# A decoder of two layers on one core: router step in three parts, roots of the low-rank rows on GpSimd, a new order table

## What is computed

```
x = LN(x + latent_attention(x))          # 32 heads, low-rank q (192) and kv (64), rotary part 64, causal
x = LN(x + mix of x with top-76-of-256 masked similarities of the context)
x = LN(x + experts(x))                   # 7 routed experts + 1 shared, top 2 of 7 by router
x = LN(x + attention(x))                 # 16 heads of 16, rotary, causal
x = LN(x + softmax(LN(sim)*gamma+beta))  # bilinear similarity with the context
x = LN(x + down(silu(gate(x)) * up(x)))  # hidden 1024
```

```
# first attention: RMS norm of the low-rank rows
q   = rms_norm(x @ q_a_w) @ q_b_w            # x * rsqrt(mean(x*x) + 1e-6) * w
ckv = rms_norm((x @ kv_a_w)[..., :64])
# router of the experts
gate = x @ Wr + br
_, ids = top_k(gate + gate_bias, 2)
masked = full(-inf); masked[ids] = gate[ids]
probs = softmax(masked)
```

## Time and profile before

| what | value |
| --- | --- |
| three runs | 713.79, 714.95, 715.62 us |
| the profiled execution | 713.86 us, of which the span from first to last instruction is 712.0 us |
| TensorE, matmuls | 686.8 us busy (96%), 4886 |
| VectorE | 539.4 us (76%), 1701 instructions |
| ScalarE | 496.5 us (70%) |
| GpSimd | 389.1 us (55%), 647 instructions |
| chain that ended last | TensorE 82%, VectorE 8%, GpSimd 3% |

### The profile page before, as it was taken

One profiled execution on the slowest core, in us unless ns is written; L12 is line 12 of the kernel. 1 busy time (PEld: TensorE's weight loads), 2 busy tenths in 40 slices (PEclk: granted clock), 3 DMA queues, 4 the chain that ended last, 5 costly groups with the idle time before them and its releaser, 6 DMA issues.

```text
span 712.0 us, 14718 instructions
## 1 busy us (share of the span) xinstructions
PE 686.8 (96%) x4886; PEld 576.6 (81%) x4886; DVE 539.4 (76%) x1701; ACT 496.5 (70%) x1277; POOL 389.1 (55%) x647
## 2 busy tenths in 40 slices
PE   8899999999999999999987999999989999999995
PEld 6577898889888888889875988888967777768885
DVE  4967899887788969888878956566788778749464
ACT  4787865888568684888877867665756676876641
POOL 4269642885267731878965546834781321336652
PEclk9999999999999999999999999999999999999998
DMA  8671001140431302212021002210120000010301
GB/s 286 172 227 34 16 1 45 46 120 1 124 114 37 114 2 65 54 33 61 1 90 46 1 0 90 77 58 1 45 89 3 4 2 4 3 46 1 122 27 45
DMA packets 34419, 41.06 MB, mean 58 GB/s; under 512 B 6620, under 2 KB 27238, under 8 KB 34344
## 3 DMA queue, kind: packets, MB, share of 16 engines
q1 hardware_dynamic: 33800, 39.80, 19.0%
q10 hardware_dynamic: 544, 0.33, 0.1%
HBM read 30.02 MB, written 1.05 MB: 44 GB/s over the span
## 4 chain that ended last, share of the span: by engine, by line
PE 82%; DVE 8%; POOL 3%; issue 2%; SPq 2%; ACT 1%; DMA 1%; POOLq 0%; DVEq 0%
PE bank L1181 72%; PE bank L1195 10%; SPq L2625 1%; DVE top_tok L2258 1%; DVE router_buf L1891 1%; POOL w_split_lo L2361 1%; POOL probs L2361 1%; POOL stat L2361 1%; DMA qT<-xT_plain 1%; DVE y L1894 1%; POOL qT L2361 0%; ACT x L1593 0%; DVE bn L1926 0%; DVE key_tok L1894 0%; DVE xT_lo L1894 0%
## 5 line engine op out<-in xcount | busy, mean ns | idle before, releaser
L2358 POOL TENSOR_SCALAR probs<-probs,soft 128x256 f32<-128x256 f32 (+1 forms) x256 | 105.7, 437 | 51.3 <-DVE soft L2054 49.8
L1681 ACT ACTIVATE probs<-probs,soft 128x256 f32<-128x256 f32 (+1 forms) x256 | 113.0, 447 | 15.1 <-DVE soft L2046 14.7
L1181 PE MATMUL bank<-xT_hi,w_split_hi 128*128 128x512 f32 x256 | 104.0, 406 | 2.5 <-POOL w_split_lo L2361 1.4
L2361 POOL TENSOR_TENSOR w_split_lo<-w_raw,w_split_hi 128x512 fp32r<-128x512 f32 (+2 forms) x57 | 73.0, 1289 | 52.3 <-ACT w_split_hi L1586 48.3
L1181 PE MATMUL bank<-xT_lo,w_split_hi 128*128 128x512 f32 x256 | 100.6, 393 | 0.0
L2046 DVE CUSTOM_DVE_ANT_0 probs<-bank,mask 128x256 f32<-128x256 f32 (+1 forms) x256 | 78.8, 353 | 25.6 <-PE bank L1181 23.7
L1181 PE MATMUL bank<-keyT,qT 128*128 128x256 f32 (+1 forms) x512 | 93.5, 330 | 2.7 <-POOL qT L2361 2.7
L1181 PEld LDWEIGHTS bank<-keyT,qT 128*128 128x128 f32 x512 | 81.9, 190 | 14.7 <-POOL qT L2361 4.8
L2361 POOL TENSOR_TENSOR qT<-qT,xT_plain 64x512 f32<-64x512 f32 x44 | 56.0, 1273 | 53.8 <-DMA qT<-xT_plain 51.6
L1181 PE MATMUL bank<-xT_hi,w_split_lo 128*128 128x512 f32 x192 | 75.7, 394 | 0.0
L1586 ACT ACTIVATE qT<-bank 64x512 f32<-64x512 f32 (+1 forms) x80 | 47.3, 593 | 29.7 <-PE bank L1181 26.3
(11 more groups left out here) (245 smaller groups left out, 1814.5 us busy)
## 6 DMA issues: line engine op xcount, KB each, us to landing
qT<-xT_plain SPq DMA_DIRECT2D x88, 64.0 KB, 2.0
w_raw<-in_w_nopeT SPq DMA_DIRECT2D x8, 512.0 KB, 3.7
w_raw_heads<-in_w_o SPq DMA_DIRECT2D x8, 512.0 KB, 5.4
qT<-rope_buf SPq DMA_DIRECT2D x40, 64.0 KB, 2.0
w_raw<-in_w_gateT SPq DMA_DIRECT2D x8, 256.0 KB, 2.7
w_raw<-in_w_upT SPq DMA_DIRECT2D x8, 256.0 KB, 3.1
w_raw<-in_w_downT SPq DMA_DIRECT2D x8, 256.0 KB, 3.7
w_raw<-in_L_ffn_Wup SPq DMA_DIRECT2D x7, 256.0 KB, 2.7
```

The source lines that it names most:

```text
L1181: return t.matmul(out, lhsT, rhs, start=start, stop=stop, skip_group_check=shared)
L1681: ins = s.activation(p[:, at], p[:, at], ACT.Exp, bias=st[:, 0, r:r + 1], scale=-1.0, accum_out=st[:, 1, r:r + 1])
L2358: return g_.tensor_scalar(out, in0, s1, s2, op0, op1)
L2361: return g_.tensor_tensor(out, in0, in1, op)
```

## The change

1. ("down_root", h): VectorE only adds the epsilon (signal `low_seeded`). GpSimd takes the power -0.5 of 8 columns and makes one Newton round of four instructions, and signals `low_rsqrt`. The step has a place in GpSimd's order, and `power` is 8 columns wide.
2. The router: the part after the top-8 search is a step of its own, ("route_pick", h), so that other steps can stand between the three parts. The second mask is added with -1 in the same instruction, and one scalar_tensor_tensor replaces the tensor_scalar and the add of route_soft: one instruction less for each half, two in all.
3. The planner's costs for these steps, `NEAR` and the table `URGENT` are new, so that every engine's order changes.
4. The two signals of the last statistics are merged with the others; their order in time is as before.

```diff
-    NEAR = {"PE": 0.0, "ACT": 0.3, "DVE": 0.3, "POOL": 0.3, "SP": 0.5, "DMA": 0.05, "WAY": 0.0}
+    NEAR = {"PE": 0.0, "ACT": 0.3, "DVE": 0.3, "POOL": 0.5, "SP": 0.3, "DMA": 0.1, "WAY": 0.0}
...
-        ("adj_T", 0): -24, ("adj_mask", 2): 70, ("adj_mask", 3, 1): 17, ("adj_sim", 2): 45, ("adj_top", 1): 362,
+        ("adj_mask", 2, 1): 49, ("adj_top", 1): 241, ("adj_top", 2): 86, ("adj_top", 3): 133, "adj_top": -33,
...
-        stage(("down_root", h), "DVE 2.7", ("down", h))
+        stage(("down_root", h), "DVE 0.2, POOL 2.2", ("down", h), ("zero",))
...
-        stage(("route_gate", h), "PE 0.5, DVE 2.7", ("route_lin", h),
+        stage(("route_gate", h), "PE 0.5, DVE 1.8", ("route_lin", h),
               holds=[bank("route_gate", h, left=(("route_gate", h), "DVE"))])
-        stage(("route_soft", h), "DVE 0.9, ACT:exp 0.3", ("route_gate", h))
+        stage(("route_pick", h), "DVE 2.2", ("route_gate", h))
+        stage(("route_soft", h), "DVE 1.8, ACT:exp 1.5", ("route_pick", h))
...
-                own(seed(ve, r, sums[:, h, :, :].rearrange("p a t -> p (a t)"), 1e-6))
-                newton_steps(ve, r, s_).then_inc(low_rsqrt.sem, 1)
+                ts(stat[place][:, 0, :], sums[:, h, :, :].rearrange("p a t -> p (a t)"), 1e-6, None, ALU.add).then_inc(low_seeded.sem, 1)
...
-                tt(pick, pick, other, ALU.add).then_inc(route_picked.sem, 1)
+
+                stt(pick, pick, -1.0, other, ALU.add, ALU.add).then_inc(route_picked.sem, 1)
...
-                own(ts(tmp, pick, -NEG, NEG, ALU.mult, ALU.add))
-                w.wait_ge(*own.now)
-                own(tt(tmp, tmp, gate, ALU.add))
+                own(stt(tmp, pick, -NEG, gate, ALU.mult, ALU.add))
...
+        def newton_step(r, s, ve):
+            w.wait_ge(*own.now)
+            own(tt(s, r, r, ALU.mult))
+            w.wait_ge(*own.now)
+            own(tt(s, s, ve, ALU.mult))
+            w.wait_ge(*own.now)
+            own(ts(s, s, -0.5, 1.5, ALU.mult, ALU.add))
+            w.wait_ge(*own.now)
+            return tt(r, r, s, ALU.mult)
...
+            elif name == "down_root":
+                h, = k
+                ve, r, s_ = (stat[in_stat.place["down", h]][:, j, :] for j in range(3))
+                w.wait_ge(*zeroed["zero"])
+                w.wait_ge(*low_seeded[h])
+                own(tt(r, ve, power[:, :], ALU.pow))
+                newton_step(r, s_, ve).then_inc(low_rsqrt.sem, 1)
```

137 lines of the change are left out of this document (54 added, 83 removed), and 41 rows, old and new, of the table URGENT.

## The result

The changed kernel takes 703.82 us (median of four runs, 702.86 to 705.43) where the kernel before took 714.37 on the same chip (713.26 to 715.62): ratio 0.9854, 95% interval 0.9828 to 0.988. Run once more on another chip it took 705.07 against 713.43, ratio 0.988 (0.9854 to 0.9905). Its profiled execution took 705.43 us with a span of 703.6 us, 8.4 less than the span of before.

What follows compares the result with a forecast made beforehand. TensorE's matmuls were taken as the bound, busy 686.8 of 712.0 us. Terms -4.2 (router), -1.2 (GpSimd's run), 0 (start), 0 (rest) sum to -5.4 us: 708.5 profiled, median 709.6, range 706.0 to 715.5.

Steps and rivals of the forecast that it cites:

- The router, -4.2: Router of half 0: xT_lo ahead of route_soft removes TensorE's 2.6 us wait and 1.7 us of low clock; -4.2 us.
- rival A: Router: the hole only moves, something else holds e_u(2,1); only GpSimd's 1.2 us left, median 713.7 us; chance 0.14.
- the new wait: Router: TensorE would wait 0.2 us for u_pair_lo, ready at 384.8 us.
- GpSimd's run, -1.2: Before the second attention: a split moved into GpSimd's idle time shortens TensorE's 1.69 us wait for q_rows; -1.2 us.
- ScalarE is late next: Before the second attention: the bound of 0 gain, if ScalarE, which makes the high part first, is late next.
- The start, 0: Roots and SP's queue: root ready as late as before, query waits may go (-2.3) or grow (+2); taken as 0.
- B: Start: SP's ten loads hold the first query beyond about 35 us; +1.7 to +3.4 us, median up to 718.3; chance 0.11.
- D: Start: GpSimd's root instructions wait for VectorE's, each root 1.8 us late, twice; -1.8 us in all, median 713.2; chance 0.07.
- C: Start: VectorE's freed 5.6 us lets first queries be evicted earlier, both query waits go; -7.7 us in all, median 707.3; chance 0.10.
- The rest of the order, 0 with a bound of -1: Some 450 steps changing places where TensorE's windows are full: 0 us, bounds -1 and +2.5.
- the price of the low clock at the router: Behind the xT_lo wait, four 1 us windows at low granted clock lack 1.7 us of full speed.

Runs made afterwards that it cites:

- fused_only: The kernel before with only the two router instructions fused away, one less per half, and nothing moved: 711.49 us against 713.38, ratio 0.9977.
- split_pair: The kernel before with the 512-wide split (17, 0) put ahead of the 1536-wide (16, 0) on ScalarE and GpSimd: 713.18 us against 713.38, ratio 0.998.
- root_on_vector: The changed kernel with the root of the low-rank rows back on VectorE and out of GpSimd's order: 705.29 us against 713.87 for the kernel before, ratio 0.9875.
- start_new: The changed kernel's instructions, its order up to about 95 us and the old order behind: 711.29 us against 713.38 for the kernel before, ratio 0.997.
- half_new: The changed kernel's instructions, its order up to the experts' end, the old order from the second attention on: 706.45 us against 713.38 for the kernel before, ratio 0.9902.
- weights_first: The changed kernel with split (10, 0) ahead of e_gate (0, 0) on ScalarE and GpSimd: 705.2 us against 713.43 for the kernel before, ratio 0.9884.
- late_new: The changed kernel's instructions, its order at the start and from the second attention on, the old order between: 707.49 us against 713.38 for the kernel before, ratio 0.9911.
- After_again: The changed kernel run once more, unchanged, on another chip: 705.07 us against 713.43 for the kernel before, ratio 0.988.
- att_new: The changed kernel's instructions, its order up to the norms behind the first attention, the old order from there: 711.36 us against 713.38 for the kernel before, ratio 0.995.
- tokens_late: The kernel before with ctx_tok's 16 small products moved later on TensorE, and their copy on VectorE: 712.94 us against 713.65, ratio 0.9983.
- xT_first: The kernel before with one VectorE step moved, batch 3's xT_lo ahead of route_soft of half 0: 710.53 us against 713.38, ratio 0.9953.

## Why the prediction was wrong, step by step

**The router, -4.2: nearly right.** The xT_lo wait and the low clock went as forecast; the step is 3.3 us in after and 3.5 for the move alone, and rival A did not come. The part mis-sized is the new wait: 0.2 forecast, 0.96 measured. I charged VectorE for GpSimd's run but not GpSimd for VectorE's: its products took 3.45 instead of 2.51 us, so the next router instruction was held as well (1.28 us). I also put the saved instruction to nothing beyond this sum. Alone the fusion is worth 2.8 us in the old order (fused_only), since it takes the wait to 1.37 us, and behind that the clock did not fall. Move and fusion cover the same hole: undoing the move costs 0.7 us with the fusion there, undoing both 1.9.

**GpSimd's run, -1.2: wrong, -0.3.** split_pair shows the step that failed: I took GpSimd's run to be bound by GpSimd alone. GpSimd also waits for VectorE's rope_tmp, 0.99 us there and 0.95 in after; the bound that I gave for "ScalarE is late next" had the right form, and VectorE was the one.

**The start, 0: near, and in part by luck.** The root is 3.1 us from the add to its end, as estimated (11.46 to 14.57), the power 1.66 and 1.85 us for an estimate of 1.7; the first query goes out at 28.38 us for a forecast 28.6; root_on_vector finds the place of the root worth nothing, which agrees with the Trainium skill (Perfetto Trace Analysis, Optimizing Scalar/DVE Operations), by which moving work between these two engines might not help. The traces of after are 0.5 and 1.8 us ahead by 348 us, and traces with the old start scatter by 1.4. The luck is in the clock: none of the six traces with the old start has it low between 14 and 75 us, six of the nine with after's start have, near 24 or 47 us, which costs 1.7 us each. The three without it (start_new, half_new, weights_first) are 1.1 to 2.4 us ahead by 348 us. So the new start takes waits away and mostly pays with the clock; I had priced neither. TensorE has 10.25 of 12 us between 36 and 48 us, its least between 24 and 60, where under 9.5 would have been the sign of B, and the first query goes out well before the 35 us of B; D's late root did not come either. Of C's two waits both went, but a new one of 1.75 us for qT came at 45.56, so C did not come as priced.

**The rest of the order, 0 with a bound of -1: the step that failed, 4.4 us.** "The largest holes of the old order outside the places above are these waits of 1.4 to 1.7 us, so I take 0": this looked for large holes in full windows. There were a wait of 1.27 us at 360.82, one of 0.74 at 373.2, and the five between 529 and 559 us. half_new gains 2.2 us at the first two, late_new 2.4 at the others and behind them, of which 0.3 is GpSimd's run. Each could have been looked up: in the listing of the new order ctx_tok stands where the hole of 1.27 us was. Which step closes each wait is shown for none of them. The sum by the traces is then -0.5 - 2.1 - 3.3 - 0.2 - 1.8 - 0.6 = -8.5, against -8.4 of the spans; without the start, the router and the 0.3 it is the 4.4 of this term.

**The clock of single executions: the last 0 to 2 us.** Executions of one kernel differ in the mean clock, and the time goes with it. Mean clock and span of seven of the 92 executions of before on record beside the experiments, and the four of after:

```
before  0.998 709.7   0.997 709.4   0.995 711.0   0.994 711.1   0.992 714.0   0.990 714.0   0.987 717.6
after   0.999 701.0   0.998 701.6   0.996 702.4   0.994 703.6
```

Over all 92 a thousandth of the clock goes with 0.68 us. 81 of them have a mean clock of 0.997, 0.995, 0.992, 0.990 or 0.987, steps of some 2.5 thousandths, which is 1.7 us of 712: an estimate from these numbers is that they count stretches like that of the earlier trace rows. The profiled execution of after was its slowest: behind the 1.75 us wait at 45.56 its clock fell, and in half_new, the same order there, behind a wait of 1.3 us it did not. The windows of after, then of half_new:

```profile
44.00:48.00 4.00, 2.44 (x12) 2.30 (x13) 1.18 (x7) 1.30 (x6) 3.76 (x7) 0.84 0.91 265
48.00:52.00 4.00, 4.00 (x17) 3.36 (x16) 2.98 (x12) 1.93 (x7) 3.84 (x7) 0.74 0.58 192
```

```profile
44.00:48.00 4.00, 2.76 (x17) 2.51 (x18) 1.79 (x10) 1.75 (x7) 3.82 (x6) 1.00 0.93 299
48.00:52.00 4.00, 4.00 (x22) 3.27 (x22) 3.60 (x18) 3.39 (x10) 3.84 (x8) 1.00 0.50 151
```

Where the stretches lie differs between executions. After_again has its own not at 47 but at 25 us:

```profile
24.00:28.00 4.00, 3.29 (x9) 2.58 (x10) 1.17 (x2) 2.07 (x5) 3.60 (x6) 0.65 0.33 68
```

Behind the q_rows wait of the second attention three of the nine traces with the old order there have one (start_new, att_new, tokens_late), 1.4 to 1.8 us each, and none of the eleven with the new order. So the new order of that stage can win more in the median than the 1.8 us, which are against an execution without it.

The mean clock is 0.9939 over the 24 executions of before beside xT_first and 0.997 over the nine of xT_first: by the 0.68 us that is 2.1 us, near the 1.7 that the four windows of the earlier trace rows lacked. So the price of the low clock at the router was right.

## What to carry to other kernels

Where a new order is part of the change, go through every wait of the old one above 0.3 us and look up in the listing what now stands before it: the waits that looked too small to price held more gain than the one that was priced. Where two edits close one hole their gains don't add up, and each is to be priced with and without the other; a move that clears a wait shows the next engine that is late (ScalarE, the other queries) at nearly the same size. Count in how many executions the clock is low at a place before you take one trace for the kernel, and look whether a kernel with the old order shows the same gain before you give it to a move. In an order this tight, five tries with one to three moves each found nothing more.

## What the runs showed of the hardware

VectorE and GpSimd hold each other: two g_pair_lo 2.93 us instead of 1.28, the two GpSimd products beside them 3.45 instead of 2.51. How the same two instructions fall together changes with the execution: 1.93 or 0.88 us for y. One instruction on 128x32, 0.19 us alone, is worth 1.22 us beside a run of GpSimd, shown by taking it out (wait 2.59 to 1.37 us).

A power of 8 columns on GpSimd takes 1.66 and 1.85 us.

The granted clock of the same place differs between executions: 0.72 at 516 to 520 us in start_new behind its 1.7 us wait for q_rows, 1.00 in before behind the same wait. A wait of 1.4 us for xT_lo at the router had no low clock behind it in any of five traces; one of 2.0 us for x had it in one of two, one of 2.6 us for xT_lo in four of five. In the new start it was low in six of nine traces, in the old one in none of six.
